# New order of the first image: loads, score rows, value tiles and weight products

## The chip, the cores and the metric

The kernel runs on one core of a Trainium2 chip. The metric is the device time of one execution in microseconds (us). Five engines work in program order, each on its own list: TensorE (PE, matrix products), VectorE (DVE), ScalarE (ACT), GpSimd (POOL) and SyncE (SP), which here only issues DMAs. They wait for one another by semaphores.

## The reference

Eight images of 256 channels by 1024 pixels go through two attention layers, all in float32.

```
# layer 0 (Cq = 32)
q = einsum('oc,bcn->bno', Wq, xf) + bq
k = einsum('oc,bcn->bon', Wk, xf) + bk[None, :, None]
v = einsum('oc,bcn->bon', Wv, xf) + bv[None, :, None]
attn = softmax(einsum('bnc,bcm->bnm', q, k), axis=-1)
x1 = gamma[0] * einsum('bcj,bij->bci', v, attn) + x
# layer 1 (C = 256, 32 groups)
h_ = group_norm(x1, norm_w, norm_b)
q, k, v = (einsum('oc,bcn->bon', w, h_) + b for q, k, v)
attn = softmax(einsum('bct,bcs->bts', q, k) * scale, axis=-1)
y = x1 + einsum('oc,bcn->bon', proj_w, einsum('bcs,bst->bct', v, attn)) + proj_b
```

## The kernel before

**Precision.** TensorE works on `fp32r` operands. Each float32 operand is split into a rounded high part and the low rest, and `three` (L596 to L599) makes a product of three matmuls: high by high, high by low, low by high. So most results on their way to TensorE are handled twice: ScalarE writes the high part, VectorE subtracts it and writes the low part.

**Layer 0 of an image** is done in two passes. First the *score tiles* `scores(i, k)` (L601), 128 queries by 1024 keys each, eight per image. VectorE takes the row maximum (`row_max`, L1062), ScalarE the exponential with its row sum (`row_sums`, L840), and the scores are thrown away. From the sums come a logarithm (`log_sums`) and a shift per query (`shifts`, L1090), which TensorE turns (`move_shift`, L631) and ScalarE copies into two rows of the query operand (`shift_rows`, L851). Then come the *key tiles* `keys(i, k)` (L610), 128 keys by 1024 queries: with the shift in the operand their exponential is the softmax already, laid out as the next product wants it. ScalarE takes the exponential and the high copy (`exponent`, `prob_hi`, L813, L826), VectorE the low part (`prob_lo`, L1078). Last `values` (L750) adds the product with the value tile into four banks of PSUM, 12 matmuls of 512 columns for each key tile, two steps behind it.

Ahead of the score tiles stand the query/key projections `qk(i, half)` (L639), whose copies go to ScalarE (`query_part`, `key_part`, L881, L889) and VectorE (L1025, L1035), and the value tiles `value0(i, m)` (L649). Image 0's value tiles are only copied out at first (ScalarE for m 0 and 1; VectorE's `keep_values`, L1049, for 2 and 3) and split later by POOL (`first_values0`, L517). `weights(0, m)` (L693) are products of layer 1's weights in float32, `bias` (L704) products of its weights and biases, 24 instructions of them with one column only. Layer 1 has logit tiles in place of score and key tiles; it follows one image behind.

**Order.** A list `STEPS` of `Step` objects, written out by hand (`first_image`, L84, and what follows), sets the order on all engines. A step has a key or logit `tile`, the sums `values` of an earlier tile, and lists `early`, `sides` and `late`. TensorE (L780 to L791) does tile, early, the first `banks_first` banks of the sums, sides, the other banks, late. ScalarE (L913 to L941) does the tile's exponential and its high copy, then early, sides, late. VectorE (L1144 to L1198) does early first, then query/key and bias entries of sides, `evacuate` where a phase ends, then the tile's low part, then the other sides and late. So the place of a score tile in the step also says whether VectorE takes its maximum ahead of or behind the low part of the key tile.

**Slots.** PSUM is a `ring` of four slots of 1024 columns; slots 2 and 3 also are the four banks of the sums. `PLACE` (L57) says which slot an entry has, else the planner takes the one given longest ago; `HOST` (L69) puts an entry in the second half of another's slot. Before it writes a slot, TensorE waits for the reader of the entry that had it (`reader`, L248). For a key tile that is ScalarE's exponential, for a score tile too, for a value tile of image 1 VectorE's low part.

**Start.** SP issues the loads one after the other (L414 to L428). TensorE runs matmuls of ones in the meantime (`keep_busy`, L591). ScalarE and VectorE split x of image 0 (`split_x`), VectorE the query/key weights (`first_weights`, L973), POOL the value weights (`small_things`, L507) and x of image 1.

Of the kernel before, what the change touches and what calls it, by code (L numbers as in the profile page):

```python
# [6 lines left out]
F32 = mybir.dt.float32  # L7
# [27 lines left out]
class Step:  # L35
# [6 lines left out]
    def __init__(self, tile=None, values=None, banks_first=2, slots=(0, 1)):  # L42
        self.tile, self.values, self.banks_first, self.slots = tile, values, banks_first, slots
        self.early, self.sides, self.late = [], [], []
        self.early_log = self.log = self.shifts = self.hidden = self.hidden_lo = self.split_x = self.x_lo_mid = self.x_lo_end = None
        self.statistics = self.evacuate = self.evacuate_at_once = None
        self.take_weights = self.keep_values = self.opening = self.rest = self.low_first = False
        self.early_in_front = False
        self.hidden_mid = None
# [7 lines left out]
PLACE = {("qk", 1, 0): 2, ("value0", 0, 2): 3, ("bias", 0, 0): 3}  # L57
PLACE.update({("weights", 0, m): 3 for m in range(4)})
PLACE.update({("keys", 0, k): 1 for k in range(2, TILES)})
PLACE.update({("scores", 1, k): 0 for k in range(7)})  # L60
# [8 lines left out]
HOST = {("qk", 1, 1): ("qk", 1, 0), ("value0", 0, 3): ("value0", 0, 2),  # L69
# [14 lines left out]
def first_image():  # L84

    start, scores, opening = Step(slots=(0, 1, 2, 3)), Step(slots=(0, 1, 2)), Step()
    start.sides = tiles("qk", 0, (0, 1)) + tiles("value0", 0, (0, 1))
    scores.late = tiles("scores", 0, (0, 1, 2)) + tiles("value0", 0, (2,)) + tiles("scores", 0, (3, 4, 5))
    scores.late += tiles("value0", 0, (3,)) + tiles("scores", 0, (6, 7))
    scores.keep_values = True  # L90
    opening.opening = True
    opening.sides = tiles("qk", 1, (0, 1))
    opening.late = tiles("shift", 0, (0,)) + tiles("weights", 0, (0,))
    steps = [Step(("keys", 0, k), (0, 0, k - 2) if k >= 2 else None) for k in range(TILES)]
    steps[0].rest = True
    steps[1].late = tiles("weights", 0, (1, 2, 3))
    steps[1].take_weights = True
    for k in range(6):
        steps[k + 2].early = tiles("scores", 1, (k,))
    steps[4].sides = tiles("value0", 1, (0,))  # L100
    steps[6].sides = tiles("value0", 1, (1,))
    steps[6].x_lo_end = 2, 0
    s8, s9, s10 = Step(None, (0, 0, 6)), Step(None, (0, 0, 7)), Step(("keys", 1, 1))
    s8.early = tiles("scores", 1, (6, 7))
    s8.early_log = 1
    s8.late = tiles("value0", 1, (2,))
    s9.sides = tiles("shift", 1, (0,))
# [159 lines left out]
def values_done(tile):  # L267
# [13 lines left out]
    "x_hi", "x_split", "res0_ready", "res1_ready", "weights_read", "weights_split", "rows_ready", "bias_read",  # L281
    "layer0_split", "v0_weights", "small_ready", "ones_ready", "key_hi", "link", "pool_link",
    "wqk_loaded", "bqk_loaded", "wv0_loaded", "weights_loaded", "x_loaded0", "x_loaded1", "x0_loaded", "y_stored")


def build(nc, x, wqk_t, bqk, bk0, wv0_t, bv0, gamma, norm_w, norm_b, wq, bq, wk, bk, wv, bv, wp_t, bp,
          ident, group, y):
    with ExitStack() as ctx:
# [124 lines left out]
        @block.sync  # L413
        def _(sp):  # L414
            for ready, loads in (
                    ("wqk_loaded", ((wqk_f, by_tile(wqk_t)),)),
                    ("x0_loaded", ((x_in[0][:, :, half_cols[0]], x_v[0][:, :, half_cols[0]]),)),
                    ("x_loaded0", ((x_in[0][:, :, half_cols[1]], x_v[0][:, :, half_cols[1]]),)),
                    ("bqk_loaded", ((bqk_s[:], bqk), (bk0_s[:], bk0))),
                    ("wv0_loaded", ((wv0_f, by_tile(wv0_t)), (bv0_s[:], bv0), (gamma_s[:], gamma),  # L420
                                    (ident_s[:], ident))),
                    ("x_loaded1", ((x_in[1][:], x_v[1]),)),
                    ("weights_loaded", ((wq_f, by_tile(wq)), (wk_f, by_tile(wk)), (wv_f, by_tile(wv)),
                                        (wp_f, by_tile(wp_t)), (bq_s[:], bq), (bk_s[:], bk),
                                        (bv_s[:], bv), (bp_s[:], bp), (nw_s[:], norm_w), (nb_s[:], norm_b),
                                        (group_s[:], group)))):
# [12 lines left out]
            sp.wait_ge(S["x_split"], 2)  # L439
            load(2)  # L440
            load(3)
            for i in range(IMAGES):
                store(i)
                if i + 4 < IMAGES:
                    load(i + 4)
            sp.wait_ge(S["y_stored"], IMAGES * BANKS * 16)

        @block.gpsimd
        def _(pool):
# [8 lines left out]
            def first_split_x():  # L458
                pool.wait_ge(x_loaded[1], x_loads(1))
                hi, lo = x_split(1)  # L460
                for half in range(HALVES):
                    cols = half_cols[half]
                    G.tensor_copy(hi[:, :, cols], x_in[1][:, :, cols]).then_inc(S["x_hi"], 1)
                    pool.wait_ge(S["x_hi"], 2 + half + 1)
                    G.tensor_tensor(lo[:, :, cols], x_in[1][:, :, cols], hi[:, :, cols].bitcast(F32),
                                    ALU.subtract).then_inc(S["x_split"], 1)
# [89 lines left out]
            pool.wait_ge(S["x0_loaded"], 16)  # L556
# [21 lines left out]
        def _(pe):  # L578
# [22 lines left out]
            def scores(i, k, out):  # L601
                if k == 0:
                    wait("qk_split", 2 * i + 2)
                    wait("key_hi", 2 * i + 2)
# [99 lines left out]
            def bias_products(slot):  # L704
                wait("rows_ready", 4)
                value_b_ps, rowk_ps, query_b_ps = bias_places(slot)
                for o in range(CT):
                    mm(value_b_ps[:, 0:C], bv_rows[:, o], wp_f[:, o], start=o == 0, stop=o == CT - 1)
# [4 lines left out]
                for ct in range(CT):  # L713
                    for out, w, b in ((rowk_ps, wq_f, bk_s), (query_b_ps, wk_f, bq_s)):
# [64 lines left out]
            keep_busy(ring[:, 3], 30)  # L779
            for now in STEPS:  # L780
                front = [now.tile] * bool(now.tile)
                for entry in now.early + front if now.early_in_front else front + now.early:
                    fill(entry)
                if now.values:
                    values(now.values, range(now.banks_first))
                for entry in now.sides:
                    fill(entry)
# [6 lines left out]
        def _(act):  # L794
            copy, activation = nc.scalar.copy, nc.scalar.activation
            nc.scalar.preload_act_table_set("natural_log_exp_and_others")

            def split_x(i):
                for half in range(HALVES):
                    cols = half_cols[half]  # L800
                    if i == 0 and half == 0:
                        act.wait_ge(S["x0_loaded"], 16)
                    else:
                        act.wait_ge(x_loaded[i % 2], x_loads(i))
# [51 lines left out]
            def project_hi(entry):  # L856
# [20 lines left out]
                if kind == "qk":  # L877
                    query_part(entry)
                    key_part(entry)
# [8 lines left out]

            def key_part(entry):  # L889
# [4 lines left out]
            def opening():  # L894
                log_sums(0)
                for m in range(2):
                    query_part(("qk", 1, m))
                shift_rows(("shift", 0, 0))
                key_part(("qk", 1, 0))
# [12 lines left out]
            split_x(0)  # L912
            for now in STEPS:  # L913
# [22 lines left out]
                if now.rest:  # L936
                    key_part(("qk", 1, 1))
# [6 lines left out]
        def _(dve):  # L944
# [13 lines left out]

            def split_x(i, half):
                cols = half_cols[half]  # L960
                dve.wait_ge(S["x_hi"], 2 * i + half + 1)
# [38 lines left out]
            def project_lo(entry):  # L1000
# [8 lines left out]
                if kind == "query":  # L1009
# [5 lines left out]
                    last.then_inc(S["query_split"], 1)  # L1015
                if kind == "value0" and i:
# [8 lines left out]
            def key_part(entry):  # L1025
                _, i, m = entry
                if i == 0 and m == 0:
# [3 lines left out]
                link(V.tensor_scalar(k[0:32, cols], out[64:96], bqk_s[64:96], None, ALU.add))  # L1031
                V.scalar_tensor_tensor(k[32:64, cols], out[64:96], bk0_s[:], k[0:32, cols].bitcast(F32),
                                       ALU.add, ALU.subtract)
# [110 lines left out]
            for now in STEPS:  # L1144
# [16 lines left out]
                if now.take_weights:  # L1161
                    take_weights()
# [28 lines left out]
                if now.keep_values:  # L1191
                    keep_values()
# [43 lines left out]
```

## Time and profile before

| | us |
|---|---|
| three timed runs, median | 789.38 |
| their lowest and highest | 786.51, 790.51 |
| the profiled execution, its own time | 785.61 |
| its span, first to last instruction | 783.8 |
| TensorE busy in the span | 774.1 (99%) |
| VectorE, ScalarE, POOL busy | 554.7, 470.7, 163.8 |
| mean granted clock of TensorE | 0.998 |

Times within the profile are counted from the start of the span. Matmuls overlap: one of 512 columns is shown with some 0.39 us, but in a row of them each starts 0.23 us after the other, so starts are what to read. A busy TensorE is not one at its best: warm-up matmuls count as busy, and at half the granted clock a matmul takes twice its time. PE stands for TensorE, DVE for VectorE, ACT for ScalarE.

### The profile page before, as it was taken

The page shows a single profiled execution, that of the slowest core. Times are in us where ns is not written, and L with a number is a line of the kernel's source. Part 1 is how long each engine was busy: PE and PEld are TensorE (multiplying, and loading weights), DVE is VectorE, ACT ScalarE, POOL GpSimd, SP SyncE. Part 2 cuts the span into 40 slices and gives each one's busy share as a digit, 9 for nine tenths or more (in the row PEclk, how much of TensorE's full clock was granted, in tenths as well). Part 3 has the DMA queues.
Part 4 walks back from the last instruction along what each step waited for, and adds up shares of the span by engine and source line. Part 5 has one row for each costly group of instructions (what it writes and reads, how often), then busy time and mean ns, then how long its engine had stood idle before and what let it go on. Part 6 is the DMA issues. An engine that isn't in the chain of part 4 may idle for free.

```text
span 783.8 us, 9844 instructions
## 1 busy us (share of the span) xinstructions
PE 774.1 (99%) x3816; PEld 647.4 (83%) x3816; DVE 554.7 (71%) x806; ACT 470.7 (60%) x619; POOL 163.8 (21%) x147
## 2 busy tenths in 40 slices
PE   9899999999999999999999999999999999999998
PEld 8678888888888888888888888888888888888886
DVE  5966778787578875788657796677856765476664
ACT  4876566567555775467745586456855566345343
POOL 5730052023100331005110240102310024111120
PEclk9999999999999999999999999999999999999999
DMA  6010010002000110001100011000100000000101
GB/s 189 0 55 1 1 54 1 1 23 86 1 1 1 55 54 1 1 1 54 55 1 1 0 56 54 1 1 0 54 1 2 0 33 22 1 0 1 54 1 54
DMA packets 10365, 18.98 MB, mean 24 GB/s; under 512 B 2128, under 2 KB 3920, under 8 KB 10320
## 3 DMA queue, kind: packets, MB, share of 16 engines
q1 hardware_dynamic: 10320, 18.36, 6.8%
q8 instruction: 30, 0.49, 0.3%
q14 instruction: 15, 0.12, 0.1%
HBM read 9.97 MB, written 8.39 MB: 23 GB/s over the span
## 4 chain that ended last, share of the span: by engine, by line
PE 95%; ACT 2%; DVE 2%; issue 0%; POOL 0%; ACTq 0%; DVEq 0%; POOLq 0%
PE ring L597 29%; PE ring L599 28%; PE ring L598 28%; PE ring L617 4%; PE ring L607 3%; PE ring L594 1%; ACT ring L844 1%; ACT pt_hi L834 1%; ACT prob L820 1%; PE ring L636 1%; DVE neg_max L1067 0%; DVE res L1120 0%; DVE pt_lo L1084 0%; PE ring L691 0%; PE ring L716 0%
## 5 line engine op out<-in xcount | busy, mean ns | idle before, releaser
L597 PE MATMUL ring<-pt_hi,v_hi 128*128 128x512 f32 x480 | 189.4, 395 | 0.0
L599 PE MATMUL ring<-pt_hi,v_lo 128*128 128x512 f32 x480 | 188.5, 393 | 0.0
L598 PE MATMUL ring<-pt_lo,v_hi 128*128 128x512 f32 x480 | 188.3, 392 | 0.0
L823 ACT ACTIVATE prob<-ring,neg_max 128x1024 f32<-128x1024 f32 x64 | 71.5, 1118 | 155.1 <-DVE neg_max L1070 155.1
L1069 DVE TENSOR_REDUCE neg_raw<-ring 128x1 f32<-128x1024 f32 x64 | 78.2, 1222 | 58.0 <-PE ring L599 57.9
L504 POOL TENSOR_TENSOR v_lo<-v_f,v_hi 128x512 fp32r<-128x512 f32 x28 | 37.7, 1347 | 385.1 <-ACT v_hi L861 385.1
L1084 DVE TENSOR_TENSOR pt_lo<-prob,pt_hi 128x1024 fp32r<-128x1024 f32 x64 | 81.8, 1278 | 37.5 <-ACT pt_hi L834 37.3
L599 PEld LDWEIGHTS ring<-pt_hi,v_lo 128*128 128x128 f32 x480 | 90.3, 188 | 19.9
L597 PEld LDWEIGHTS ring<-pt_hi,v_hi 128*128 128x128 f32 x480 | 90.5, 188 | 18.4 <-issue 0.4
L598 PEld LDWEIGHTS ring<-pt_lo,v_hi 128*128 128x128 f32 x480 | 90.6, 189 | 18.2
L1067 DVE TENSOR_REDUCE neg_max<-ring 128x1 f32<-128x1024 f32 x64 | 77.7, 1223 | 35.4 <-PE ring L607 35.3
L844 ACT ACTIVATE ring<-ring,neg_max 128x1024 f32<-128x1024 f32 x64 | 69.4, 1084 | 39.9 <-DVE neg_max L1067 39.8
L1087 DVE SCALAR_TENSOR_TENSOR pt_lo<-prob,row_inv,pt_hi 128x1024 fp32r<-128x1024 f32 x64 | 83.1, 1298 | 8.6 <-ACT pt_hi L837 8.4
L597 PE MATMUL ring<-h_hi,query_hi 128*128 128x512 f32 x224 | 88.0, 393 | 0.0
L598 PE MATMUL ring<-h_lo,query_hi 128*128 128x512 f32 x224 | 87.5, 391 | 0.0
L599 PE MATMUL ring<-h_hi,query_lo 128*128 128x512 f32 x224 | 87.5, 391 | 0.0
L820 ACT ACTIVATE prob<-ring 128x1024 f32<-128x1024 f32 x64 | 65.5, 1024 | 36.4 <-PE ring L617 36.2
L837 ACT ACTIVATE pt_hi<-prob,row_inv 128x1024 fp32r<-128x1024 f32 x64 | 73.7, 1152 | 9.6 <-DVE row_inv L1076 9.3
L834 ACT CAST pt_hi<-prob 128x1024 fp32r<-128x1024 f32 x64 | 67.3, 1051 | 5.3
L599 PEld LDWEIGHTS ring<-h_hi,query_lo 128*128 128x128 f32 x224 | 42.0, 188 | 8.9
L597 PEld LDWEIGHTS ring<-h_hi,query_hi 128*128 128x128 f32 x224 | 42.1, 188 | 8.8 <-ACT prob L823 0.2
L598 PEld LDWEIGHTS ring<-h_lo,query_hi 128*128 128x128 f32 x224 | 42.1, 188 | 8.6
(167 smaller groups left out, 1346.8 us busy)
## 6 DMA issues: line engine op xcount, KB each, us to landing
out_y<-res SPq DMA_DIRECT2D x32, 256.0 KB, 2.2
x_in<-in_x SPq DMA_DIRECT2D x7, 1024.0 KB, 4.9
x_in<-in_x SPq DMA_DIRECT2D x2, 512.0 KB, 5.2
h_f<-in_wv_t SPq DMA_DIRECT2D x1, 256.0 KB, 4.4
res<-in_wq SPq DMA_DIRECT2D x1, 256.0 KB, 6.8
res<-in_wk SPq DMA_DIRECT2D x1, 256.0 KB, 7.1
res<-in_wv SPq DMA_DIRECT2D x1, 256.0 KB, 7.6
res<-in_wp_t SPq DMA_DIRECT2D x1, 256.0 KB, 7.1
```

The source lines that it names most:

```text
L597: mm(out, w_hi, m_hi, start=first, stop=False)
L598: mm(out, w_hi, m_lo, start=False, stop=False)
L599: return mm(out, w_lo, m_hi, start=False, stop=last)
L820: activation(prob[:, p % PROBS], ring[:, slot], ACT.Exp).then_inc(S["keys_exp"], 1)
L823: activation(prob[:, p % PROBS], ring[:, slot], ACT.Exp, bias=neg_max[:, k % 2:k % 2 + 1], accum_out=row_sum[:, k % 2:k % 2 + 1]).then_inc ...
L834: copy(pt_hi[p % PT][:], prob[:, p % PROBS]).then_inc(S["p_hi"], 1)
L837: activation(pt_hi[p % PT][:], prob[:, p % PROBS], ACT.Identity, scale=row_inv[:, k % 2:k % 2 + 1]).then_inc(S["p_hi"], 1)
L844: activation(ring[:, slot], ring[:, slot], ACT.Exp, bias=neg_max0[:, k:k + 1], accum_out=row_sum0[:, k:k + 1]).then_inc(S["scores_exp"], 1)
L1067: V.tensor_reduce(neg_max0[:, k:k + 1], src, AX_X, ALU.max, negate=True).then_inc(S["scores_max"], 1)
L1069: link(V.tensor_reduce(neg_raw[:, k % 2:k % 2 + 1], src, AX_X, ALU.max, negate=True))
L1084: V.tensor_tensor(lo[:], src, hi[:].bitcast(F32), ALU.subtract).then_inc(S["p_split"], 1)
L1087: V.scalar_tensor_tensor(lo[:], src, row_inv[:, k % 2:k % 2 + 1], hi[:].bitcast(F32), ALU.mult, ALU.subtract).then_inc(S["p_split"], 1)
```

## The change

- *Loads.* The first half of x of image 0 is loaded first, in two DMAs of one channel tile each, then the query/key weights, the small query/key biases, the second half of x. ScalarE and VectorE split x of image 0 in four parts of 128x512; VectorE does the weights between the two halves.
- *Warm-up.* 18 passes for 30.
- *First score tiles.* `scores(0, 0)` to `(0, 3)` wait for the first half of the queries and all keys only. For qk(0,1) ScalarE writes the high keys (`first_key_part`) and its query part last.
- *Entries of the first steps.* Value tile (0,1) moves between score tiles 2 and 3, (0,2) into the opening, (0,3) behind keys(0,1), the weight products among score tiles 5 to 7. qk(1,0) comes behind the shift, qk(1,1) behind keys(0,0).
- *Score tiles of image 1.* Tiles 0 to 5 were early in steps 2 to 7. Now tiles 0, 1, 2 are late in steps 3, 4, 5, tile 3 is in the sides of step 6, tile 4 in those of step 7, tile 5 late in step 7. Tiles 6 and 7 come behind three banks of the sums in the step after. Value tile (1,2) moves into the last step of the sums.
- *Slots* are given by hand where they weren't.
- *Bias products.* The eight one-column products with `bk_s` come first, and each half of the 256-column products goes ahead of eight one-column instructions.

```
-PLACE = {("qk", 1, 0): 2, ("value0", 0, 2): 3, ("bias", 0, 0): 3}
+PLACE = {("qk", 0, 0): 1, ("qk", 0, 1): 0, ("value0", 0, 0): 3, ("value0", 0, 2): 0, ("qk", 1, 0): 2, ("shift", 0, 0): 1,
+         ("keys", 0, 0): 1, ("keys", 0, 1): 3, ("bias", 0, 0): 3}
+PLACE.update({("scores", 0, k): (2, 1, 0)[k % 3] for k in range(TILES)})
 PLACE.update({("weights", 0, m): 3 for m in range(4)})
 PLACE.update({("keys", 0, k): 1 for k in range(2, TILES)})
-PLACE.update({("scores", 1, k): 0 for k in range(7)})
+PLACE.update({("scores", 1, k): int(k in (5, 7)) for k in range(TILES)})
...
-HOST = {("qk", 1, 1): ("qk", 1, 0), ("value0", 0, 3): ("value0", 0, 2),
+HOST = {("qk", 1, 1): ("qk", 1, 0), ("value0", 0, 1): ("value0", 0, 0), ("value0", 0, 3): ("value0", 0, 2),
...
-    start, scores, opening = Step(slots=(0, 1, 2, 3)), Step(slots=(0, 1, 2)), Step()
-    start.sides = tiles("qk", 0, (0, 1)) + tiles("value0", 0, (0, 1))
-    scores.late = tiles("scores", 0, (0, 1, 2)) + tiles("value0", 0, (2,)) + tiles("scores", 0, (3, 4, 5))
-    scores.late += tiles("value0", 0, (3,)) + tiles("scores", 0, (6, 7))
-    scores.keep_values = True
+    start, scores, opening = Step(), Step(), Step()
+    start.sides = tiles("qk", 0, (0, 1)) + tiles("value0", 0, (0,))
+    scores.late = tiles("scores", 0, (0, 1, 2)) + tiles("value0", 0, (1,)) + tiles("scores", 0, (3, 4, 5))
+    scores.late += tiles("weights", 0, (0,)) + tiles("scores", 0, (6,)) + tiles("weights", 0, (1,))
+    scores.late += tiles("scores", 0, (7,)) + tiles("weights", 0, (2, 3))
     opening.opening = True
-    opening.sides = tiles("qk", 1, (0, 1))
-    opening.late = tiles("shift", 0, (0,)) + tiles("weights", 0, (0,))
+    opening.sides = tiles("value0", 0, (2,))
+    opening.late = tiles("shift", 0, (0,)) + tiles("qk", 1, (0,))
     steps = [Step(("keys", 0, k), (0, 0, k - 2) if k >= 2 else None) for k in range(TILES)]
-    steps[0].rest = True
-    steps[1].late = tiles("weights", 0, (1, 2, 3))
-    steps[1].take_weights = True
-    for k in range(6):
-        steps[k + 2].early = tiles("scores", 1, (k,))
+    steps[0].late = tiles("qk", 1, (1,))
+    steps[1].late = tiles("value0", 0, (3,))
+    for k, s in enumerate((3, 4, 5)):
+        steps[s].late = tiles("scores", 1, (k,))
     steps[4].sides = tiles("value0", 1, (0,))
-    steps[6].sides = tiles("value0", 1, (1,))
+    steps[6].sides = tiles("value0", 1, (1,)) + tiles("scores", 1, (3,))
     steps[6].x_lo_end = 2, 0
-    s8, s9, s10 = Step(None, (0, 0, 6)), Step(None, (0, 0, 7)), Step(("keys", 1, 1))
+    steps[7].sides, steps[7].late = tiles("scores", 1, (4,)), tiles("scores", 1, (5,))
+    s8, s9, s10 = Step(None, (0, 0, 6), 3), Step(None, (0, 0, 7)), Step(("keys", 1, 1))
+    s8.early_behind = True
     s8.early = tiles("scores", 1, (6, 7))
     s8.early_log = 1
-    s8.late = tiles("value0", 1, (2,))
-    s9.sides = tiles("shift", 1, (0,))
+    s9.sides = tiles("value0", 1, (2,)) + tiles("shift", 1, (0,))
     s9.late = tiles("keys", 1, (0,))
     s10.sides = tiles("bias", 0, (0,))
...
+                    ("x0_loaded0", ((x_in[0][:, 0, half_cols[0]], x_v[0][:, 0, half_cols[0]]),)),
+                    ("x0_loaded1", ((x_in[0][:, 1, half_cols[0]], x_v[0][:, 1, half_cols[0]]),)),
                     ("wqk_loaded", ((wqk_f, by_tile(wqk_t)),)),
-                    ("x0_loaded", ((x_in[0][:, :, half_cols[0]], x_v[0][:, :, half_cols[0]]),)),
+                    ("bqk_loaded", ((bqk_s[:], bqk), (bk0_s[:], bk0))),
                     ("x_loaded0", ((x_in[0][:, :, half_cols[1]], x_v[0][:, :, half_cols[1]]),)),
-                    ("bqk_loaded", ((bqk_s[:], bqk), (bk0_s[:], bk0))),
...
-                if k == 0:
+                if (i, k) == (0, 0):
+                    wait("qk_split", 1)
+                    wait("key_first", 1)
+                    wait("key_lo", 1)
+                    wait("key_hi", 2)
+                elif k == 0 or (i, k) == (0, TILES // 2):
                     wait("qk_split", 2 * i + 2)
                     wait("key_hi", 2 * i + 2)
...
-                for o in range(CT):
-                    mm(value_b_ps[:, 0:C], bv_rows[:, o], wp_f[:, o], start=o == 0, stop=o == CT - 1)
                 for j in range(2):
                     for o in range(CT):
                         mm(value_b_ps[:, C + j:C + j + 1], bq_rows[:, o], bk_s[:, o:o + 1],
                            start=o == 0, stop=o == CT - 1)
                 for ct in range(CT):
+                    cols = slice(ct * P, (ct + 1) * P)
+                    for o in range(CT):
+                        mm(value_b_ps[:, cols], bv_rows[:, o], wp_f[:, o, cols], start=o == 0, stop=o == CT - 1)
...
-            keep_busy(ring[:, 3], 30)
+            keep_busy(ring[:, 3], 18)
...
                 for entry in now.early + front if now.early_in_front else front + now.early:
-                    fill(entry)
+                    if not (now.early_behind and entry in now.early):
+                        fill(entry)
                 if now.values:
                     values(now.values, range(now.banks_first))
+                if now.early_behind:
+                    for entry in now.early:
+                        fill(entry)
...
+            def first_split_x():
+                for half in range(HALVES):
+                    for ct in range(CT):
+                        if half == 0:
+                            act.wait_ge(S[("x0_loaded0", "x0_loaded1")[ct]], 16)
+                        else:
+                            act.wait_ge(x_loaded[0], x_loads(0))
+                        copy(x_hi[:, ct, half_cols[half]], x_in[0][:, ct, half_cols[half]]).then_inc(S["x0_hi"], 1)
...
-                    query_part(entry)
-                    key_part(entry)
+                    if (i, m) == (0, 1):
+                        first_key_part(entry)
+                        key_part(entry)
+                        query_part(entry)
+                    else:
+                        query_part(entry)
+                        key_part(entry)
...
+            def first_key_part(entry):
+
+                act.wait_ge(S["ring_ready"], RING_NO[entry] + 1)
+                activation(k4[0][0:32, half_cols[entry[2]]], half_place(entry)[64:96], ACT.Identity,
+                           bias=bqk_s[64:96]).then_inc(S["key_first"], 1)
...
                 log_sums(0)
-                for m in range(2):
-                    query_part(("qk", 1, m))
                 shift_rows(("shift", 0, 0))
+                query_part(("qk", 1, 0))
                 key_part(("qk", 1, 0))
...
+                first_split_x(0)
                 dve.wait_ge(S["wqk_loaded"], 16)
                 split(wqk_hi[:], wqk_lo[:], wqk_f).then_inc(S["layer0_split"], 1)
-                for half in range(HALVES):
-                    split_x(0, half)
+                first_split_x(1)
...
+                if entry == ("value0", 0, 3):
+                    keep_values()
...
+                if (i, m) == (0, 1):
+                    dve.wait_ge(S["key_first"], 1)
+                else:
+                    link(V.tensor_scalar(k[0:32, cols], out[64:96], bqk_s[64:96], None, ALU.add))
+                last = V.scalar_tensor_tensor(k[32:64, cols], out[64:96], bk0_s[:], k[0:32, cols].bitcast(F32),
+                                              ALU.add, ALU.subtract)
+                if (i, m) == (0, 1):
+                    last.then_inc(S["key_lo"], 1)
...
                 shifts(0)
-                for m in range(2):
-                    key_part(("qk", 1, m))
-                for m in range(2):
-                    query_part(("qk", 1, m))
+                take_weights()
+                key_part(("qk", 1, 0))
+                query_part(("qk", 1, 0))
...
-                if now.take_weights:
-                    take_weights()
...
-                if now.keep_values:
-                    keep_values()
```

## Rows read from the trace of the kernel before

**Rows 1.** Windows by stage: length, busy time (instructions) of each engine, mean granted clock, DMA.
```profile
0.00:15.00 15.00, 14.02 (x96) 13.26 (x96) 7.16 (x10) 6.69 (x8) 6.95 (x15) 1.00 0.83 243
15.00:38.30 23.30, 19.73 (x97) 15.03 (x97) 20.41 (x24) 19.58 (x29) 18.67 (x17) 1.00 0.01 2
38.30:71.10 32.80, 30.86 (x154) 24.67 (x153) 22.19 (x24) 22.23 (x31) 7.37 (x7) 1.00 0.10 33
71.10:80.00 8.90, 8.90 (x49) 7.59 (x49) 6.22 (x13) 6.11 (x6) 0.00 (x0) 0.81 0.01 2
80.00:765.00 685.00, 684.98 (x3358) 574.33 (x3358) 489.15 (x726) 410.23 (x539) 130.81 (x110) 1.00 0.05 19
```

**Rows 2.** The waits up to 80 us: waited for, total us, times, longest.
```profile
PE ring L607 <- ACT ring L844: 2.7, 5, 1.5
```

**Rows 3.** Timeline of TensorE: start, length, line, operands, count [idle before].
```profile
0.98 8.39 PE L594 MATMUL ring<-ones 128*128 128x128 f32 x60 [0.98 <-POOL unit L544]
9.12 0.48 PE L597 MATMUL ring<-x_hi,wqk_hi 128*128 128x512 f32 x1
...
12.01 0.28 PE L597 MATMUL ring<-wv_hi,x_hi 128*128 128x256 f32 x1
...
14.71 0.28 PE L599 MATMUL ring<-wv_hi,x_lo 128*128 128x256 f32 x1
15.74 1.62 PE L607 MATMUL ring<-k,q 96*128 96x512 f32 x6 [0.75 <-DVE q L1039]
...
35.56 0.40 PE L597 MATMUL ring<-pt_hi,v_hi 128*128 128x512 f32 x1
...
38.30 0.63 PE L617 MATMUL ring<-q,k 98*128 98x512 f32 x2
...
70.93 1.09 PE L617 MATMUL ring<-q,k 98*128 98x512 f32 x4
...
72.91 0.95 PE L711 MATMUL ring<-bk_s,bq_rows 128*128 128x1 f32 x8
```

**Rows 4.** Windows of one microsecond, behind the one-column matmuls.
```profile
76.00:77.00 1.00, 1.00 (x4) 0.81 (x3) 0.93 (x7) 0.33 (x1) 0.00 (x0) 0.50 0.00 0
```

**Rows 5.** Timeline of ScalarE.
```profile
7.49 1.05 ACT L805 CAST x_hi<-x_in 128x1024 fp32r<-128x1024 f32 x1 [0.46 <-DMA x_in<-in_x]
...
17.73 1.09 ACT L844 ACTIVATE ring<-ring,neg_max 128x1024 f32<-128x1024 f32 x1 [2.12 <-DVE neg_max L1067]
...
27.56 0.21 ACT L849 ACTIVATE log_sum<-row_sum 128x8 f32<-128x8 f32 x1
...
29.20 1.00 ACT L854 CAST q<-ring 2x1024 fp32r<-2x1024 f32 x1 [0.29 <-PE ring L636]
...
39.13 1.09 ACT L844 ACTIVATE ring<-ring,neg_max 128x1024 f32<-128x1024 f32 x1 [1.09 <-DVE neg_max L1067]
...
40.23 1.02 ACT L820 ACTIVATE prob<-ring 128x1024 f32<-128x1024 f32 x1
...
53.78 1.03 ACT L820 ACTIVATE prob<-ring 128x1024 f32<-128x1024 f32 x1 [0.71 <-PE ring L617]
54.90 1.05 ACT L834 CAST pt_hi<-prob 128x1024 fp32r<-128x1024 f32 x1
...
66.84 0.21 ACT L849 ACTIVATE log_sum<-row_sum 128x8 f32<-128x8 f32 x1
```

**Rows 6.** Timeline of VectorE.
```profile
2.93 0.29 DVE L954 TENSOR_SCALAR wqk_hi<-h_f 128x256 fp32r<-128x256 f32 x1 [2.93 <-DMA h_f<-in_wqk_t]
...
16.48 6.88 DVE L1067 TENSOR_REDUCE neg_max<-ring 128x1 f32<-128x1024 f32 x6 [0.99 <-PE ring L607]
...
55.98 1.22 DVE L1084 TENSOR_TENSOR pt_lo<-prob,pt_hi 128x1024 fp32r<-128x1024 f32 x1 [0.86 <-ACT pt_hi L834]
...
69.06 2.83 DVE L1117 SCALAR_TENSOR_TENSOR x<-ring,gamma_s,x 128x512 f32<-128x512 f32 x4
```

**Rows 7.** Timeline of POOL.
```profile
10.35 1.28 POOL L513 TENSOR_TENSOR wv_lo<-h_f,wv_hi 128x512 fp32r<-128x512 f32 x1
```

More of the change, by code:

```diff
@@ L46, in __init__ @@
         self.statistics = self.evacuate = self.evacuate_at_once = None
-        self.take_weights = self.keep_values = self.opening = self.rest = self.low_first = False
-        self.early_in_front = False
+        self.opening = self.low_first = False
+        self.early_in_front = self.early_behind = False
         self.hidden_mid = None
@@ L280 @@
     "v1_full", "v1_hi", "value1_split", "stats_ready", "norm_read", "coef_ready", "h_full", "h_hi", "h_split",
-    "x_hi", "x_split", "res0_ready", "res1_ready", "weights_read", "weights_split", "rows_ready", "bias_read",
+    "x0_hi", "x_hi", "x_split", "key_first", "key_lo", "res0_ready", "res1_ready", "weights_read", "weights_split", "rows_ready", "bias_read",
     "layer0_split", "v0_weights", "small_ready", "ones_ready", "key_hi", "link", "pool_link",
-    "wqk_loaded", "bqk_loaded", "wv0_loaded", "weights_loaded", "x_loaded0", "x_loaded1", "x0_loaded", "y_stored")
+    "wqk_loaded", "bqk_loaded", "wv0_loaded", "weights_loaded", "x_loaded0", "x_loaded1", "x0_loaded0", "x0_loaded1", "y_stored")
 def build(nc, x, wqk_t, bqk, bk0, wv0_t, bv0, gamma, norm_w, norm_b, wq, bq, wk, bk, wv, bv, wp_t, bp,
@@ L463, in first_split_x @@
                     G.tensor_copy(hi[:, :, cols], x_in[1][:, :, cols]).then_inc(S["x_hi"], 1)
-                    pool.wait_ge(S["x_hi"], 2 + half + 1)
+                    pool.wait_ge(S["x_hi"], half + 1)
                     G.tensor_tensor(lo[:, :, cols], x_in[1][:, :, cols], hi[:, :, cols].bitcast(F32),
@@ L555, in _ @@
             pool.wait_ge(S["value0_first"], 4)
-            pool.wait_ge(S["x0_loaded"], 16)
+            pool.wait_ge(S["x0_loaded0"], 16)
+            pool.wait_ge(S["x0_loaded1"], 16)
             pool.wait_ge(x_loaded[0], x_loads(0))
@@ L796, in _ @@
             nc.scalar.preload_act_table_set("natural_log_exp_and_others")
+            def first_split_x():
[6 more added lines that the diff above has]
+                        copy(x_hi[:, ct, half_cols[half]], x_in[0][:, ct, half_cols[half]]).then_inc(S["x0_hi"], 1)
             def split_x(i):
+                act.wait_ge(x_loaded[i % 2], x_loads(i))
                 for half in range(HALVES):
                     cols = half_cols[half]
[L801 to L804, printed above, removed]
                     copy(x_hi[:, :, cols], x_in[i % 2][:, :, cols]).then_inc(S["x_hi"], 1)
@@ L910, in follow @@
                     project_hi(entry)
-            split_x(0)
+            first_split_x()
             for now in STEPS:
@@ L935, in _ @@
                     log_sums(now.log)
-                if now.rest:
-                    key_part(("qk", 1, 1))
                 if now.split_x is not None:
@@ L957, in _, with first_split_x @@
             scale = C ** -0.5
+            def first_split_x(half):
+                cols = half_cols[half]
+                for ct in range(CT):
+                    dve.wait_ge(S["x0_hi"], CT * half + ct + 1)
+                    last = V.tensor_tensor(x_lo[:, ct, cols], x_in[0][:, ct, cols], x_hi[:, ct, cols].bitcast(F32),
+                                           ALU.subtract)
+                last.then_inc(S["x_split"], 1)
             def split_x(i, half):
                 cols = half_cols[half]
-                dve.wait_ge(S["x_hi"], 2 * i + half + 1)
+                dve.wait_ge(S["x_hi"], 2 * (i - 1) + half + 1)
                 V.tensor_tensor(x_lo[:, :, cols], x_in[i % 2][:, :, cols], x_hi[:, :, cols].bitcast(F32),
@@ L1030, in key_part @@
                 k, cols, out = k4[i % 2], half_cols[m], half_place(entry)
-                link(V.tensor_scalar(k[0:32, cols], out[64:96], bqk_s[64:96], None, ALU.add))
-                V.scalar_tensor_tensor(k[32:64, cols], out[64:96], bk0_s[:], k[0:32, cols].bitcast(F32),
-                                       ALU.add, ALU.subtract)
+                if (i, m) == (0, 1):
[6 more added lines that the diff above has]
+                    last.then_inc(S["key_lo"], 1)
             def query_part(entry):
```

## The prediction

> **What bounds the kernel now.** I read the windows first: from 80 to 765 us TensorE is busy 684.98 of 685.00 us, so nothing there can be won, and a delay that enters before it is never made good [rows 1]. The change touches what lies before: in the 71.1 us up to the first key tile of image 1, TensorE is idle 15.00-14.02, 23.30-19.73 and 32.80-30.86, together 6.5 us [rows 1]. The waits name the releasers: the score matmuls (L607) waited 2.7 us for ScalarE's exponentials of scores (L844), in 5 waits of which the longest was 1.5 us [rows 2]. Two losses are no idle time. Until 9.12 us TensorE runs warm-up matmuls [rows 3], and after the 24 one-column matmuls that start at 72.91 us (8 of L711, 16 of L716) the granted clock is at its lower level, 1.2 GHz (0.50) [rows 3, 4]. The stretch from 71.1 to 80 us has a mean of 0.81: 8.9 x 0.19 = 1.7 us lost, some 3.4 us at half speed [rows 1].
>
> My unit of account is the start of keys(1,0), 70.93 us before [rows 3]: in both orders the same matmuls have been done by then. Below, step n is the step of keys(0,n).
>
> **The change part by part, as a walk in time.** Durations and hand-overs are those of the rows before.
>
> *Loads and x split.* Half 1 of x reached ScalarE at 7.49 us [rows 5]. The bytes up to it are the same in the new order, so I leave it there. The query/key weights now come behind the first half of x. They had been seen at 2.93 us [rows 6], as the first load. As third they come between there and 7.49; even in proportion to the bytes (640 of 1152 KB) it is 5 to 6 us. Behind their split (two instructions, the first 0.29 us, [rows 6]) qk(0,0) can start between 6 and 7.3 us instead of 9.12 [rows 3]. The 18 warm-up passes (30 took 8.14 us, the first ones slower) end near 6.4, so they don't hold it. The parts of half 1 are finished on VectorE at about 9.5, qk(0,1) runs to 11.0. But value tile (0,0) waits for the value weights of POOL, done at 10.35+1.28 = 11.63 [rows 7]; their last load is issued one place later, whose bytes in front are unchanged: 11.65 to 12.2. A value tile is 12 matmuls, 24 took 12.01 to 14.99: 1.4 us [rows 3]. The first score tile so starts at 13.2 (its other waits: query split 11.75, key_lo 12.5) against 15.74 [rows 3]. Gain there 2.5 us, between 1.8 and 3.
>
> *First score phase.* The exponentials before ran from 17.73, one each 1.15 us, to the logarithm at 27.56 [rows 5]. Now they start at 15.2; ScalarE has 8 of them and the copy of value tile (0,1), 0.6 us, between: 15.2+9.2+0.6 = 25.0. The weight products lie in TensorE's waits for these exponentials (4 x 1.0 us), and take their slot 3 only. Gain 2.5 us kept.
>
> *Opening, steps 0 to 2.* Logarithm to shift copy took 29.20-27.56 = 1.64 us and the copy 1.0 [rows 5]; now the copy is at 26.6 to 27.6. ScalarE then still has qk(1,0), whose matmuls come behind the shift (28.05), two parts of 0.70: the first exponential of keys is at 29.5. Then come its rounding copy, the two parts of qk(1,1) that used to be ahead or later, and exponential (0,1) at 33.0. VectorE is the worse one: behind the low part of keys(0,0), at 31.65, it has key (0.75+0.75) and query (0.75) of qk(1,1), and ends at 35.1. The value sums of tile 0 need that slot. They start at 35.2, against 35.56 [rows 3]. Of the 2.5 us 0.4 is left, and score tile (1,0), 0.5 us of TensorE, is not done yet. So at step 3 the new order is level: 37.95 us against 38.30 [rows 3].
>
> *Score rows of image 1 from "early" to "late" and "sides".* This decides. Before, VectorE took the row maximum ahead of the low part of the key tile. Now a late score tile is taken behind it, and ScalarE, which works in program order, may not begin the next key exponential before that score exponential. The loop in steps 3 to 7 is one serial chain: key exponential to rounding copy 54.90-53.78 = 1.12; copy to low part 55.98-54.90 = 1.08; low part to maximum 1.15 (the pitch in the row of six); maximum to its exponential 17.73-16.48 = 1.25; that to the next key exponential 40.23-39.13 = 1.10 [rows 5, 6]. Sum 5.7 us a step. TensorE needs 2.74+0.47+0.47 = 3.7 us in a step (12 value matmuls from 35.56 to 38.30, [rows 3]), 5.1 with a value tile. It is coupled by slot 1: value tile (1,0) in step 4 and (1,1) in step 6 need the key exponential of their own step. Walking on:
> - key exponential 3 at 38.6; score tile (1,0) on TensorE 41.15; low part 40.8, maximum 41.95, its exponential 43.2; key exponential 4 at 44.3.
> - value tile (1,0) could start at 43.5 and starts at 45.4: 1.9 us idle. Sums end 48.2, score tile (1,1), maximum 48.9, exponentials 50.15 and 51.25 (key 5). One loop more: key 6 at 56.95, against 53.78 [rows 5].
> - value tile (1,1) could start at 54.2, starts at 58.05: 3.85 us idle. Its low part is ahead of the maximum of (1,3) at 61.0; key 7 at 63.35, TensorE waits 0.3 us.
> - step 7 has two score tiles behind one low part (65.55): maxima 66.7 and 67.85, exponentials 67.95 and 69.1. They free the slots for tiles 6 and 7 at 69.1 and 70.25; three banks of sums cover until 67.8; idle 1.3+0.7. Their exponentials are at 71.15 and 72.3, the logarithm at 73.5, against 66.84 [rows 5].
> - in the step after, value tile (1,2) is taken by VectorE only behind the evacuation of all four banks, the last two of which come behind the shift: sums end 76.35, last bank evacuated 77.2 (four took 2.83 us), low part 0.7 [rows 6]. keys(1,0), in the same slot, at 77.95: 1.6 us idle, where before none was.
>
> So +7.0 us at keys(1,0) (77.95-70.93). Counter-sum: TensorE's work from step 3 to there is 5 key tiles, 28 banks of sums, 8 score tiles, 3 value tiles and the shift, 30.1 us; the new stretch is 40.0 us, the listed idle times 9.9. Bounds of this term: if each hand-over is 0.1 us quicker or slower, 25 of them in the chain give 2.5 us, thus +4.5 to +9.5.
>
> *Bias products.* The eight one-column products stay at 0.81 us; the wide ones are halved and put between the two groups of eight instructions, their number of columns is the same: 0 (at most 0.2). No row shows what the clock does then. Either it stays up, -1.7 us, or nothing changes, 0. I take -1.7, since no longer run of small matmuls than 0.9 us is left.
>
> *POOL and the later loads.* Value tiles 2 and 3 are kept at 37.5 us instead of next to the first shift, so POOL's residual of image 0 and behind it, on SP, the load of x(2) come some 6 us later, near 45. Its split is first wanted at 62: hidden by 10 us. Uncovered it would delay keys(1,0) one for one.
>
> Sum: +7.0-1.7 = +5.3 us on 785.61 us (the profiled execution; its span is 783.8, rounding and start around it 1.8), 790.9. The median of the timed runs is 789.38, 3.8 above the profiled one; +5.2 on it is 794.6.
>
> **Rivals.**
> 1. *The clock falls in the new idle time*, or doesn't rise at the bias products. Speaks for it: 3.85 us of idle TensorE in one piece, where the longest wait up to now is 1.5 us [rows 2] and was survived at 1.00. Price: 3.4 us at half speed, of which 0.3 is hidden: +1.4; with the bias products as before +1.7 more. 796.0 to 797.7. The Trainium skill, "TensorE: Matmul & The Clock Gate", section "HAM oscillation — how this bites in real kernels", says that the array loses its full clock in a long idle gap and begins the next work at half rate. By it this rival would be the rule at step 6. The trace here shows such a fall only behind the one-column matmuls; no row has an idle gap this long.
> 2. *The serial loop binds only in part*: TensorE is so late in a step that the maximum finds the low part long done. Then one of the two large stalls goes (3.85), and it's +1.4: 790.8. Against it: VectorE's low part starts when ScalarE's copy ends, not when TensorE does.
> 3. *Faster:* the 2.5 us of the opening are kept and the clock repaired, -4.1: 785.3. That needs key exponential 6 ahead of 54.2 us, the point at which TensorE asks for the slot, three microseconds ahead of my walk. VectorE would have to be free for qk(1,1) before key exponential 0 as before.
> 4. *The new bias order repairs no clock*, all else as forecast: +7.0, 796.4.
>
> **How the numbers follow.** Forecast 0.50 (its own range 792 to 797), rival 1 0.16, rival 2 0.16, rival 3 0.10, rival 4 0.08. About 0.5%, 3.9 us, is what a measurement here can tell from no change. Slower by more: most of the forecast (0.39), 1 and 4: 0.63. Within: the rest of the forecast (0.11), rival 2 (0.13) and a little of 3 (0.02): 0.26. Faster by more: 0.11, with rival 3 and a part of 2 where both stalls go. The range for 8 in 10 reaches from between rivals 3 and 2 to beyond rival 1: 787 to 799.5.
>
> **What would show it.** First score matmul at 13.2 us; logarithm at 25.0; key exponentials of steps 3 to 7 about 5.7 us apart or more; TensorE idle before the value tiles of image 1 (1.9 and 3.9 us), released by ScalarE's L820 line; keys(1,0) released by VectorE's low part of a value tile; granted clock 1.00 behind the bias products. Wrong it would be above all if key exponential 6 comes before 55 us, or if TensorE's idle time from step 3 to keys(1,0) is below 7 us in sum.

## The result

The changed kernel took 801.25 us in the median of 4 runs (800.59 to 804.86) against 788.64 (786.51 to 790.51): ratio 1.0159, 95% interval 1.0113 to 1.0205, some 12.5 us slower. In a second series, taken on one chip together with some of the variants below (a2_changed), it was 802.50 against 787.55, ratio 1.0184 (1.0160 to 1.0209). Slower was forecast, with 794.6 us; the time lies above the range, and the loss is 2.4 times the forecast 5.2 us.

The profile after is of an execution of 804.86 us, the slowest of the changed kernel on record; the one before, of 785.61 us, is among the fastest of its kernel. Its page, parts 1 and 2, and then windows by stage with the columns of [rows 1]:

```profile
PE 783.6 (98%) x3796; PEld 655.0 (82%) x3796; DVE 554.7 (69%) x807; ACT 472.0 (59%) x622; POOL 162.1 (20%) x147
...
PEclk9898799999999999999999999999999999999999
```

```profile
15.00:34.40 19.40, 17.91 (x91) 14.31 (x90) 13.78 (x17) 14.81 (x24) 11.40 (x11) 0.91 0.03 6
...
37.70:44.00 6.30, 6.28 (x15) 4.95 (x16) 3.29 (x3) 1.59 (x2) 3.91 (x4) 0.51 0.00 0
44.00:87.00 43.00, 34.06 (x154) 26.89 (x152) 22.93 (x24) 22.48 (x31) 9.73 (x9) 0.92 0.08 25
87.00:102.00 15.00, 15.00 (x67) 13.61 (x68) 7.28 (x14) 6.94 (x8) 0.00 (x0) 0.66 0.00 1
...
120.00:780.00 660.00, 659.98 (x3240) 553.69 (x3239) 471.47 (x699) 395.98 (x521) 127.17 (x104) 1.00 0.06 20
```

Behind 120 us the kernel is as full as before. Ahead of it two things are new. TensorE is idle 8.9 of the 43 us from 44 to 87, where it was idle 1.9 of 32.8 [rows 1]. And the third number from the right, the granted clock, is under 1 in each of these stages up to 102 us: in all it is at 0.50 for 27.3 us, against 3.4. Half of that is the most it can cost, up to 13.7 us against 1.7. In windows of a quarter of a microsecond there are five falls: from 20.0 us for 3.4 us, from 37.0 for 6.8, from 64.3 for 3.4, from 78.0 for 3.4, from 88.3 for 10.2.

The waits of TensorE up to 120 us show who it was idle for (before: [rows 2]):

```profile
PE ring L601 <- ACT prob L840: 6.1, 2, 3.5
PE ring L601 <- DVE q L1082: 3.2, 1, 3.2
PE ring L616 <- ACT ring L864: 2.6, 5, 1.0
PE ring L626 <- DVE v_lo L1057: 1.4, 1, 1.4
PE ring L601 <- DVE x_lo L991: 1.1, 1, 1.1
```

The timeline of TensorE, whose rows answer to [rows 3]:

```profile
0.98 6.83 PE L598 MATMUL ring<-ones 128*128 128x128 f32 x36 [0.98 <-POOL unit L547]
7.56 0.48 PE L601 MATMUL ring<-x_hi,wqk_hi 128*128 128x512 f32 x1
...
14.00 1.71 PE L616 MATMUL ring<-k,q 96*128 96x512 f32 x6
...
37.72 0.76 PE L601 MATMUL ring<-pt_hi,v_hi 128*128 128x512 f32 x1 [3.18 <-DVE q L1082]
...
42.98 1.05 PE L626 MATMUL ring<-q,k 98*128 98x512 f32 x2
...
51.64 0.39 PE L601 MATMUL ring<-wv_hi,h_hi 128*128 128x256 f32 x1 [2.54 <-ACT prob L840]
...
64.33 0.57 PE L601 MATMUL ring<-wv_hi,h_hi 128*128 128x256 f32 x1 [3.53 <-ACT prob L840]
...
86.96 1.20 PE L626 MATMUL ring<-q,k 98*128 98x512 f32 x4 [1.44 <-DVE v_lo L1057]
```

One turn of the loop in steps 5 and 6, on ScalarE, then on VectorE:

```profile
57.58 1.02 ACT L840 ACTIVATE prob<-ring 128x1024 f32<-128x1024 f32 x1
58.68 1.05 ACT L854 CAST pt_hi<-prob 128x1024 fp32r<-128x1024 f32 x1
62.16 1.09 ACT L864 ACTIVATE ring<-ring,neg_max 128x1024 f32<-128x1024 f32 x1 [2.43 <-DVE neg_max L1109]
...
63.26 1.01 ACT L840 ACTIVATE prob<-ring 128x1024 f32<-128x1024 f32 x1
```

```profile
59.76 1.23 DVE L1126 TENSOR_TENSOR pt_lo<-prob,pt_hi 128x1024 fp32r<-128x1024 f32 x1 [3.33 <-ACT pt_hi L854]
60.91 1.22 DVE L1109 TENSOR_REDUCE neg_max<-ring 128x1 f32<-128x1024 f32 x1
```

From key exponential to key exponential 63.26-57.58 = 5.68 us; the walk had 5.7. This is the one turn where nothing else comes in. The key exponentials 3 to 7 start at 44.12, 50.58, 57.58, 63.26 and 70.87 us: 6.46, 7.00, 5.68 and 7.61 apart, 26.75 in all, where the walk had 24.75. The second holds a value tile's copy in the walk too (6.95).

### The profile page after: what moved, and what is told of

It is laid out like the page before. It is cut to its first block, busy times and chain, and to the rows that moved or that the text cites. A ratio compares the mean times of both kernels' runs of the same rounds, so it can differ in the third digit from the quotient of the medians.

```text
span 803.1 us, 9813 instructions
## 1 busy us (share of the span) xinstructions
PE 783.6 (98%) x3796; PEld 655.0 (82%) x3796; DVE 554.7 (69%) x807; ACT 472.0 (59%) x622; POOL 162.1 (20%) x147
## 4 chain that ended last, share of the span: by engine, by line
PE 92%; DVE 3%; ACT 3%; issue 1%; DMA 1%; SPq 0%; ACTq 0%; DVEq 0%
PE ring L601 28%; PE ring L603 28%; PE ring L602 28%; PE ring L626 3%; PE ring L616 3%; DVE neg_max L1109 1%; ACT ring L864 1%; ACT prob L840 1%; DVE pt_lo L1126 1%; DMA x_in<-in_x 1%; ACT pt_hi L854 1%; PE ring L645 0%; PE ring L726 0%; PE ring L710 0%; DVE res L1162 0%
```

## The experiments

Each was timed beside the kernel before. Ratios with 95% intervals; "low" is the mean over the runs of (1 - granted clock) x span, an upper bound of what the recorded low clock took; "rest" is the mean time less low. For the kernel before, rest is 784.5, 784.9 and 785.3 on the three chips used, so between rows from different chips a difference in rest of under 1 us says nothing.

| kernel | ratio to before | low | rest |
|---|---|---|---|
| before (69 runs, mean 787.4) | 1 | 2.4 | 785.0 |
| changed (9 runs, mean 802.0) | 1.0159, 1.0184 | 11.7 | 790.4 |
| e1_early | 1.0058 (1.0039 to 1.0076) | 5.9 | 785.5 |
| e2_late_only | 1.0094 (1.0077 to 1.0111) | 4.2 | 789.6 |
| e3_bias_only | 1.0009 (0.9991 to 1.0028) | 2.7 | 785.3 |
| e4_start_only | 0.9991 (0.9975 to 1.0006) | 3.1 | 783.6 |
| e6_early_v12 | 1.0023 (1.0006 to 1.0040) | 5.1 | 784.5 |
| e7_v12_back | 1.0142 (1.0118 to 1.0165) | 7.6 | 790.5 |
| e5_fill, f2_fill | 1.0164 (1.0143 to 1.0186), 1.0159 (1.0133 to 1.0185) | 7.0 | 792.8 |
| e10_bias_apart | 1.0004 (0.9991 to 1.0016) | 2.3 | 785.1 |
| e8_gaps | 0.9974 (0.9957 to 0.9992) | 1.6 | 784.0 |
| e9_gaps_bias | 0.9983 (0.9973 to 0.9994) | 1.4 | 784.1 |

A tenth run of the changed kernel, outside the median and the nine, took 797.65 us at a mean clock of 0.991; with it the mean is 801.6.

**Score rows, from both sides.** e1_early undoes them in the changed kernel, e2_late_only does them alone.

```
e1: steps[3..7].early = scores(1, 0..4); steps[7].late = scores(1, 5)
e2: the kernel before + PLACE, late/sides of scores(1, k) and s8 as changed
```

> The changed kernel, but score tiles (1,0) to (1,4) are early in steps 3 to 7, so VectorE takes their maximum ahead of the low part of the key tile; tile (1,5) and all else as changed. Theory L (serial loop): steps 3 to 7 are set by TensorE again, key exponentials 6 and 7 come 3.5 us or more sooner counted from exponential 3, the waits of 2.5 and 3.5 us ahead of value tiles (1,0) and (1,1) are gone, and with them the fall of the clock at 64 us: 6 to 12 us faster than the changed kernel, about 791 us. Rival S (the start and the opening lose it, the score rows are hidden): within 2 us of the changed kernel, 799 to 801.

> The kernel before, and only the score tiles of image 1 moved as in the change (late in steps 3 to 5, sides in 6 and 7, late in 7, tiles 6 and 7 behind three banks). Theory L: the loop of 5.7 us a step costs 5 to 7 us of idle TensorE, and the idle time lets the clock fall once or twice, 1.7 us each, at other places than before: 7 to 10 us slower than before. Rival S: within 2 us of before.

Undone, 1.0184 or 1.0159 becomes 1.0058: 8 to 10 us back. Alone they cost 7.4 us. TensorE's wait for the key exponentials is in e2_late_only and not in e1_early; first the waits of e2_late_only with its key exponentials 5 to 7, then the two longest waits of e1_early:

```profile
PE ring L599 <- ACT prob L826: 5.1, 2, 3.4
...
51.00 1.01 ACT L826 ACTIVATE prob<-ring 128x1024 f32<-128x1024 f32 x1
56.68 1.01 ACT L826 ACTIVATE prob<-ring 128x1024 f32<-128x1024 f32 x1
...
63.54 1.01 ACT L826 ACTIVATE prob<-ring 128x1024 f32<-128x1024 f32 x1
```

```profile
PE ring L601 <- DVE q L1082: 3.2, 1, 3.2
PE ring L626 <- DVE v_lo L1057: 2.2, 2, 1.4
```

Again 5.68 us from 5 to 6. Rest moves by 4.9 and 4.6 us in the two experiments (4.2 and 5.1 when each is set against the kernel before on its own chip); the remainder is low. Rival S falls. The low clock of the parts doesn't add up: against before it is 1.8 us more with the score rows alone, 3.5 us more with all else, 9.2 us more with both.

**The clock, with more work.** e5_fill adds 38 products with zeros in TensorE's idle time; f2_fill is the same kernel beside a2_changed, the changed kernel, on one chip.

```
+ mm(out, zeros_r[...], moving, start=False, stop=...)  # x12 in keys(0,2), x11 in step 4, x15 in step 6
```

> The changed kernel plus 38 matmuls of 512 columns whose stationary operand is all zeros, accumulated into places in use, so that they add nothing: 12 with key tile (0,2), 11 in step 4 and 15 in step 6, where TensorE sat idle 3.2, 2.5 and 3.5 us. The chain of the other engines is as changed. Theory C (idle time of TensorE makes the granted clock fall and that is some 5 to 10 of the 12.5 us): the falls at 37 and 64 us are gone, and with 38 matmuls more the kernel is 3 to 7 us faster than the changed one. Rival N (the clock isn't governed by this idle time, or its falls are hidden in the waits): the same time or up to 2 us slower.

> The changed kernel itself, once more, on the chip of e4_start_only and e6_early_v12, for their differences. 800 to 802 us; the sum of low clock stays about 20 to 27 us of its profile.

> e5_fill itself, once more, beside the changed kernel on one chip. Theory C: 2 to 5 us faster than a2_changed, with 38 matmuls more. Rival N: no faster.

The walk's main stretch, from the first sums to keys(1,0), is in the window of f2_fill, then of a2_changed:

```profile
36.20:80.20 44.00, 40.53 (x193) 32.16 (x193) 25.50 (x27) 24.23 (x33) 14.66 (x12) 1.00 0.08 25
```

```profile
36.70:82.90 46.20, 38.78 (x167) 30.76 (x167) 25.04 (x27) 24.05 (x33) 14.59 (x12) 0.89 0.07 23
```

With 26 of the added matmuls in it, the stretch is 2.2 us shorter, and the clock is 1.00 where it was 0.89. The timed runs show less. e5_fill was expected 3 to 7 us faster than the changed kernel; its ratio, 1.0164, is not under the 1.0159 of the first series: a miss. f2_fill is at the lower end of what was expected, 800.12 against 802.50 us on the same chip, and the intervals of the two ratios overlap (1.0133 to 1.0185, 1.0160 to 1.0209). Low is 4.7 us less, rest 2.4 us more (on that chip alone 4.1 and 2.1): that the zeros aren't all hidden is the likely reason, not shown by itself. So that filling the waits holds the clock up stands on the profiles and on low; that it makes this kernel faster is not shown. Behind 84 us the clock falls in f2_fill as well; there nothing was filled. The runs of the changed kernel say without any edit that low clock is lost time: 797.65 us at a mean clock of 0.991, 799.87 at 0.989, 804.86 at 0.983, 7.2 us from first to last for 6.5 us of low. Over the 69 runs of the kernel before, time grows by 0.81 us for each us of low (correlation 0.83).

**Value tile (1,2).** e7_v12_back undoes its move alone, e6_early_v12 on top of e1_early.

```
- s9.sides = tiles("value0", 1, (2,)) + tiles("shift", 1, (0,))
+ s8.late = tiles("value0", 1, (2,)); s9.sides = tiles("shift", 1, (0,))
```

> The changed kernel with only value tile (1,2) back ahead of the last sums, so that its low part on VectorE comes before the evacuation. Theory W: the wait of 1.4 us ahead of keys(1,0) goes, 1 to 3 us faster than the changed kernel (of the difference between e6_early_v12 and e1_early, 2.8 us by the medians' ratios, part was the clock). Rival: the wait only moves to the next step, no gain.

> The changed kernel with score tiles (1,0) to (1,4) early, as e1_early, and value tile (1,2) back ahead of the last sums. Theory W: the wait of 1.4 us ahead of keys(1,0) for VectorE's low part goes, and with it perhaps part of the fall of the clock behind it: 1.4 to 4 us faster than e1_early, 788 to 790. Rival: VectorE was late for keys(1,0) anyway, the same as e1_early.

By the ratios e7_v12_back is 1.3 to 3.3 us faster than the changed kernel and e6_early_v12 2.8 us faster than e1_early; in both pairs the intervals overlap, and neither pair ran on one chip. Rest of e7_v12_back is that of the changed kernel, 790.5, so its gain is low clock. The wait ahead of keys(1,0) is gone in its profile, but half of it is back as a wait of 0.7 us ahead of value tile (1,2):

```profile
PE ring L602 <- ACT ring L865: 0.7, 1, 0.7
```

In e6_early_v12 rest is 0.9 us less than in e1_early, and 1.8 less when each is set against before on its own chip: there the wait may have cost time of its own. In the profile of e7_v12_back the 15 us behind keys(1,0) run at full clock, where the changed kernel had 0.66:

```profile
84.50:99.50 15.00, 15.00 (x88) 12.91 (x88) 12.18 (x23) 10.37 (x12) 0.00 (x0) 1.00 0.00 1
```

**The bias products.** e3_bias_only has the new order alone; e10_bias_apart puts a key tile between the one-column instructions.

```
e10: bias_first(slot)   # 256-column products, 8 one-column
     keys(1, 2)
     bias_products(slot)  # 16 one-column
```

> The kernel before with nothing but the new order of the bias products. If a shorter run of one-column matmuls keeps the clock up: granted clock 1.00 at 76 us and 1.7 us less, 0.2% faster. If that order doesn't matter: the clock falls all the same and the time is that of before, within 0.3 us in the profiled stretch.

> The kernel before, with key tile (1,2) put between the 8 and the 16 one-column instructions of the bias products (the 256-column ones stay ahead of the 8). Theory: the fall at 76 us comes from the run of one-column instructions; broken by a real tile it is rarer or shorter, up to 1.7 us faster than before. Rival (as e3_bias_only): any order of these 24 leaves the fall, the time is that of before.

Neither moved the time. The clock fell in the profile of both behind these products, for 6.8 us instead of 3.4; the windows of e3_bias_only, then of e10_bias_apart:

```profile
71.00:85.00 14.00, 14.00 (x77) 12.14 (x76) 8.92 (x16) 7.65 (x8) 0.00 (x0) 0.76 0.01 2
```

```profile
71.00:83.00 12.00, 12.00 (x58) 10.58 (x57) 7.05 (x14) 6.59 (x7) 0.00 (x0) 0.72 0.01 1
```

**The start, and a version that beats both.** e4_start_only is the kernel before with the loads, the x parts, 18 warm-up passes, first keys and first score phase. e8_gaps keeps TensorE at work in its waits; e9_gaps_bias adds e10's order.

```
e8: e4 with keep_busy(ring[:, 3], 20) for 18
+ if entry == ("qk", 0, 1): keep_busy(ring[:, 3], 4)
+ if entry == ("value0", 0, 0): keep_busy(ring[:, 2], 3)
```

> The kernel before with only the start and the first score phase of the change: x first and in parts, 18 warm-up passes, the waits and parts of the first keys, value tile (0,0) ahead of the scores, (0,1), (0,2), (0,3) among them, slots of the score tiles by hand. Weight products, opening and all later steps as before. Theory W (the walk: the start alone is a gain and is lost in the opening behind it): first score tile near 14 us instead of 15.74, logarithm near 26 instead of 27.56, key tile (0,0) about 1 us earlier, and the whole 0.5 to 1.5 us faster than before as long as the clock doesn't fall. Rival S (waits at the start let the clock fall and that costs more than it gives): a fall near 20 us, as fast as before or up to 3 us slower.

> e4_start_only with TensorE kept at work in the waits of the start: 20 warm-up passes for 18, 4 passes of the same kind ahead of qk(0,1) and 3 ahead of value tile (0,0). Theory C (idle time at the start lets the clock fall at 11 and 21 us): these falls are rarer, and the median comes nearer to the fastest run of e4_start_only, 783 to 785.5, faster than before. Rival: the falls come from the waits between the score tiles, which stay: 786.5 like e4_start_only.

> e8_gaps and e10_bias_apart together, the version that should beat both kernels if both theories hold: 782 to 785 us, 0.3 to 0.6% faster than before. If neither holds: 786 to 788.

e4_start_only is the same as before; its fastest run, 783.26 us at clock 1.00, is 2.2 us under the fastest of before. Its profile lost the clock twice in the first 30 us. The profile of e8_gaps shows no fall at all, and it is faster than both kernels, 785.74 us, ratio 0.9974, if just above the 783 to 785.5 us that were expected. Its interval overlaps that of e4_start_only, so what the filled waits alone give is not shown clear of noise; low is 1.6 us against 3.1. Windows of e4_start_only, then of e8_gaps:

```profile
0.00:15.00 15.00, 11.88 (x60) 10.66 (x61) 6.28 (x10) 6.78 (x10) 6.97 (x15) 0.89 0.78 243
15.00:30.00 15.00, 13.13 (x64) 10.31 (x63) 11.46 (x12) 10.95 (x21) 8.70 (x7) 0.89 0.02 3
```

```profile
0.00:15.00 15.00, 13.96 (x83) 12.76 (x84) 7.30 (x12) 7.60 (x11) 6.61 (x15) 1.00 0.81 243
15.00:38.30 23.30, 20.50 (x106) 15.54 (x105) 20.74 (x24) 19.61 (x29) 19.26 (x17) 1.00 0.01 2
...
71.10:80.00 8.90, 8.90 (x58) 7.84 (x57) 6.23 (x13) 6.71 (x7) 0.00 (x0) 1.00 0.01 2
```

The bias order adds nothing to it (0.9983, 785.67 us; 782 to 785 were expected). The gain of e8_gaps, 0.1 to 0.4%, is small, and a part of it, 1.0 us of rest, is the start that the change had right.

## Why the prediction was right or wrong

- *The loop of the late score rows* was right in mechanism and nearly in size: 5.68 us in the undisturbed turn for 5.7, 26.75 us from key exponential 3 to 7 for 24.75; waits of 2.54 and 3.53 us at the two value tiles for 1.9 and 3.85; 4.6 to 4.9 us of rest in the experiments. Idle time of TensorE from 44 to 87 us is 8.9 us for a predicted 9.9 from step 3 on (the waits that the walk lists add up to 9.65, not 9.9).
- *keys(1,0)* came at 86.96 us, +16.0, where the walk had +7.0. The low clock up to there, 17.1 us of it, is up to 8.5 us. What is left, +7.5, fits the walk. In the profile of a2_changed it came at 82.88, +12.0, with 10.2 us of low clock ahead of it, up to 5.1: +6.8 is left. In f2_fill's, with no low clock ahead of it, it came at 80.18, +9.25, the zeros included. Over the timed runs rest rose by 5.4 us, which, as low is an upper bound, is the least that isn't recorded low clock. With the 0.81 us of time for each us of low of the kernel before, an estimate is 7.5 us for the clock and 7.2 for all else, the waiting above all.
- *The failed step* is the clock. The sum took -1.7 us for the bias products, as if the clock had one cause in one place, and rival 1 priced one further fall at +1.4 and gave it 0.16. Low clock rose from 2.4 to 11.7 us in the mean, +9.2 us, and the profile has five falls where one was priced at most. The second of them lasted 6.8 us and not 3.4, and 12 matmuls of sums in it took 42.98-37.72 = 5.26 us, where they took 2.74 [rows 3]: 2.5 us, where rival 1 had 1.4 for a fall. With +9.2 in place of -1.7 the sum would be 16, against 14.7 between the means of all runs (low is an upper bound: part of it falls in waits). The rule of the Trainium skill cited there, "TensorE: Matmul & The Clock Gate", section "HAM oscillation — how this bites in real kernels", that a long idle gap costs the array its full clock, pointed the right way. This case's trace agrees with it for two falls of the five: from 37.0 us, in the wait of 3.18 us that ends at 37.72, and from 64.3 us, at the end of the one of 3.53. The walk's own numbers left 2.9 us of idle time ahead of the first sums (matmuls of 4.2 us behind 28.05, sums at 35.2), and it wasn't listed as a place where the clock could fall. The other three, 17 of the 27.3 us, stand behind no such wait: at 20.0 us behind waits of 0.3 to 0.4 us between score tiles, at 78.0 behind waits of 1.04 and 0.39, at 88.3 behind a wait of 1.44 and in the one-column products. Why the clock falls there stays open.
- *The start:* 14.0 us for the first score tile against 13.2. The warm-up matmuls ran to 7.56 us, not 6.4, and so did hold the first projection, against what the walk says; the second half of x reached ScalarE at 8.34 us, not 7.49; and value tile (0,0) waited for its weights until 12.48. Each is small. The first logarithm was at 27.3, not 25.0: the clock was at 0.50 from 20.0 to 23.4 us, from just ahead of the first float32 weight product (20.54) on, and with it these products and score tile 6 ran slower.
- *Value tile (1,2):* the wait was there, 1.44 us for 1.6, but taken out of the changed kernel it gave back no rest (e7_v12_back), and on top of e1_early 0.9 to 1.8 us of it. So as a term of 1.6 us of its own it isn't confirmed; in the changed kernel the gain was low clock.
- *Bias products:* I took the best case for -1.7 us; no order tried here repaired it. But the clock is 1.00 there in e8_gaps with the old order, in e7_v12_back with the new one, and over the whole execution in 6 of the 69 runs of the kernel before. So these products can run without a fall, and one profile with a fall behind them was too little to price it. Rival 3 adds 2.5 and 1.7 to 4.1; the sum is 4.2, which changes nothing.

## What to carry to other kernels

In a program of in-order engines, ask of each moved entry what it now stands behind on the *second* engine: a row maximum behind the low part closed a ring of five hand-overs, 5.7 us, around a step that needs 3.7. When a walk finds idle time of TensorE of some microseconds, price it twice, as waiting and as clock: here the two were of about the same size by the estimate above. Filling a wait with matmuls that do nothing went with a higher mean clock where it was tried (f2_fill, e8_gaps); whether it saves time has to be timed, for in f2_fill half of the gain in low went into rest. And one profile is one execution: where runs of one kernel differ by 5 us with the clock, compare low over many runs before giving a stretch of low clock a price.

## What the runs showed of the hardware

One kernel's time goes with its mean granted clock from run to run: before, 785.5 us in the mean of 6 runs at 1.000 and 789.5 of 9 runs at 0.993. It isn't all: 31 runs at 0.998 reach from 785.58 to 788.83.

At the start the matmuls speed up at different times, and the record doesn't show it. The same 30 warm-up passes ended at 9.12 us in the profile before and at 10.02 in e3_bias_only's. From 1 to 4 us 5 to 7 of their matmul rows start in a microsecond, later 12, and the change comes at 4 us in one and at 6 in the other, while the row of the granted clock has 1.00 throughout. So low holds nothing of the start, and rest does.

Why the clock falls in one execution and not in the next is open.
